# Transformer layers on one core: the expert phase between the two shared halves of each FFN, all routing inside the first half, and no engine loops

## The reference

```python
x = x + 0.5 * _L0_ffn_ref(_layernorm(x, axis=-1), ...)
x = x + _L0_attn_ref(_layernorm(x, axis=-1), ...)
x = x + 0.5 * _L0_ffn_ref(_layernorm(x, axis=-1), ...)
```

```python
xn = xf * jax.lax.rsqrt(jnp.mean(xf * xf, axis=-1, keepdims=True) + eps)
probs = jax.nn.softmax(xn @ router_w.T, axis=-1)
topk_p, topk_i = jax.lax.top_k(probs, K)              # K = 2 of E = 8 experts
order = jnp.argsort(~sel, axis=1, stable=True)
dispatch = order[:, :capacity]                        # 640 slots for each expert
eout = jnp.einsum('eci,eih->ech', gate * up, rd)      # 1024 hidden channels
routed = jnp.zeros_like(xf).at[dispatch.reshape(-1)].add(contrib.reshape(-1, h))
```

## Time and profile before

| | before |
|---|---|
| timed runs, median | 2442.22 us (2438.7 to 2442.6) |
| span of the profiled execution | 2445.0 us |
| PE busy | 2300.4 us (94%) |
| DVE busy | 1379.4 us (56%) |
| POOL busy | 501.5 us (21%) |

### The profile page before, as it was taken

The page is one execution under the profiler, slowest core; times in us unless marked ns, Lnnn a source line. Parts: engine busy times, 40 slices in busy tenths (PEclk is TensorE's granted clock), DMA queues, the critical chain, the costliest instruction groups (busy, mean ns, idle before and its releaser), DMA issues. The chain is left out here.

```text
span 2445.0 us, 42873 instructions
## 1 busy us (share of the span) xinstructions
PE 2300.4 (94%) x14276; PEld 2116.3 (87%) x14276; DVE 1379.4 (56%) x2890; ACT 970.2 (40%) x1940; POOL 501.5 (21%) x614
## 2 busy tenths in 40 slices
PE   7999999998999997788888988999999998999997
PEld 6888888887999997688888877888888887999997
DVE  4554454433666666778777773554454433666663
ACT  3333333332444444545444542333333332544442
POOL 1000003442121122223222220000003443121222
PEclk9999999998999999778787787999999998999999
DMA  6212113422343443100000002212113422343441
GB/s 207 72 59 87 61 57 107 126 81 72 94 104 91 99 99 90 61 1 0 0 0 0 0 1 87 76 56 87 61 57 109 124 80 68 98 103 89 102 92 17
DMA packets 198241, 175.59 MB, mean 72 GB/s; under 512 B 18697, under 2 KB 176829, under 8 KB 198144
## 3 DMA queue, kind: packets, MB, share of 16 engines
q1 hardware_dynamic: 177152, 144.57, 19.4%
q0 software_dynamic: 20992, 29.77, 6.4%
HBM read 108.51 MB, written 72.26 MB: 74 GB/s over the span
## 5 line engine op out<-in xcount | busy, mean ns | idle before, releaser
L340 PE MATMUL gate_p<-zh,w 128*128 128x320 f32 (+1 forms) x2048 | 641.3, 358 | 3.3 <-DVE zl L845 3.3
L340 PE MATMUL quad<-zh,w 128*128 128x320 f32 (+1 forms) x2048 | 628.8, 352 | 0.0
L1032 DVE TENSOR_TENSOR h_s<-quad,sg_s 128x512 f32<-128x512 f32 (+1 forms) x512 | 302.2, 590 | 473.9 <-PE quad L340 467.0
L658 ACT CAST hh<-h_s 128x512 fp32r<-128x512 f32 (+1 forms) x512 | 276.4, 540 | 648.9 <-DVE h_s L1032 648.9
L1040 DVE TENSOR_TENSOR hl<-h_s,hh 128x512 fp32r<-128x512 f32 (+1 forms) x512 | 303.8, 593 | 305.1 <-ACT hh L658 305.1
L649 ACT ACTIVATE sg_s<-gate_p 128x512 f32<-128x512 f32 (+1 forms) x512 | 265.2, 518 | 414.7 <-PE gate_p L340 414.5
L377 PE MATMUL quad<-w,hh 128*128 128x256 f32 x2048 | 410.2, 283 | 3.9 <-DVE hl L1040 3.9
L340 PEld LDWEIGHTS quad<-zh,w 128*128 128x128 f32 x2048 | 375.6, 189 | 44.2
L340 PEld LDWEIGHTS gate_p<-zh,w 128*128 128x128 f32 x2048 | 377.5, 189 | 40.3 <-DVE zl L845 3.7
L340 PE MATMUL gate_p<-zl,w 128*128 128x512 f32 (+1 forms) x1024 | 361.7, 353 | 0.0
L340 PE MATMUL quad<-zl,w 128*128 128x512 f32 (+1 forms) x1024 | 360.0, 352 | 0.0
(11 more groups left out here) (179 smaller groups left out, 3002.1 us busy)
## 6 DMA issues: line engine op xcount, KB each, us to landing
stage<-in_L_ffn_rg SPq DMA_DIRECT2D x128, 128.0 KB, 2.3
stage<-in_L_ffn_ru SPq DMA_DIRECT2D x128, 128.0 KB, 2.4
stage<-in_L_ffn_rd SPq DMA_DIRECT2D x128, 128.0 KB, 2.3
slots_d<-empty SPq DMA_DIRECT2D x16, 662.5 KB, 4.8
xr<-slots_d SPq DMA_DIRECT2D x32, 265.0 KB, 3.0
zh_d<-zh SPq DMA_DIRECT2D x16, 512.0 KB, 3.1
zl_d<-zl SPq DMA_DIRECT2D x16, 512.0 KB, 3.9
zn_d<-zn SPq DMA_DIRECT2D x16, 512.0 KB, 5.1
```

The lines of the kernel that those rows point to most:

```text
L340: last = pe.matmul(dst, a, b, start=(k == 0), stop=(k == 3 * n - 1))
L658: nc.scalar.copy(hh[:, par, 0:ncol], h_s[:, par, 0:ncol]).then_inc(sm["hh_done"], 1)
L1032: v.tensor_tensor(h_s[:, par, 0:ncol], up_p[:, par, 0:ncol], sg_s[:, par, 0:ncol], ALU.mult).then_inc(sm["h_done"], 1)
```

## The change

The phases of each FFN now run in the order `s0`, `e`, `s1`. The preparation of a block is spread over three chunks, so that all eight blocks are prepared by chunk 23 of the 64 chunks of `s0`; blocks 2 to 7 are prepared in separate buffers (`zph`, `zpl`), saved, and loaded back for their own `s0` block. The 15 parts of routing run at chunks 24 to 34 of `s0`, most of them two to a chunk. `scatter` has four row buffers and loads rows three tiles ahead. The expert sums of both FFNs are added in an internal array; `x` is loaded back during `s1`, and `s1` adds its shared half to it. In FFN 2 the finished `x` is then saved as the output. The attention weights are loaded and split, and most padding is cleared, during `s1` of FFN 1; the two value buffers are cleared by POOL after the last down matmul. All loops are written out. The first weights of FFN 2 are split during the last block of `s1`.

```diff
-        PH = {"s0": 0, "s1": NB, "e": 2 * NB}
+        PH = {"s0": 0, "e": NB, "s1": NB + NEB}
+        def prep_at(g):
+            k, r = divmod(g + 2, 3)
+            return (k, ("ln", "rows", "T")[r]) if 1 <= k < NB else (None, None)
+        def router_at(g):
+            k, r = divmod(g - 2, 3)
+            return k if r == 0 and 1 <= k < NB else None
+        ROUTE_M = 30
+        ROUTE = {24: (0,), 25: (1,), 26: (3, 4), 27: (5, 6), 28: (7,), 31: (8, 9), 32: (10, 11), 33: (12, 13), 34: (14, 15)}
...
-                for phase in ("s0", "s1", "e"):
-                    period = 4 if phase == "e" else 2
+                for phase in ("s0", "e", "s1"):
+                    if phase == "e":
+                        row_transposes(f, 0)
...
+                                for part in ROUTE.get(g, ()):
+                                    route(f, part)
+                                if c == 6:
+                                    piece_low(f, 1, b)
...
+            def row_load(f, t):
+                q = t % SROWS
+                wait(pool, scat[q], 32 * (NT // SROWS * f + t // SROWS))
+                g.dma_start(srow[:, q, 0:C], zn_rows[:, t, :]).then_inc(sr_in[q], 16)
+                g.tensor_copy(srow[:, q, C:ROW], table[:, t, :])
+                g.tensor_copy(sidx[:, q, :], slot_i[:, :, t]).then_inc(sm["sidx_in"], 1)
+            def scatter(f):
+                for t in range(SROWS - 1):
+                    row_load(f, t)
+                for t in range(NT):
+                    q = t % SROWS
+                    if t + SROWS - 1 < NT:
+                        row_load(f, t + SROWS - 1)
+                    pool.wait_ge(sr_in[q], 16 * (NT // SROWS * f + t // SROWS + 1))
...
             def attention():
+                pool.wait_ge(sm["down_done"], NCH * FB)
+                g.memset(vh[:, :, :, :].bitcast(F32), 0.0).then_inc(sm["a_const"], 1)
+                g.memset(vl[:, :, :, :].bitcast(F32), 0.0).then_inc(sm["a_const"], 1)
...
+            def shared_phase_1(f):
+                load_z(f, "s1", 1)
+                for par in range(2):
+                    sp.wait_ge(sadd[par], 48 * XB * (f + 1))
+                for b in range(NB):
+                    load_sums(f, b)
+                for b in range(NB):
+                    if b + 1 < NB and b:
+                        load_z(f, "s1", b + 1)
...
+                    if f == 0 and b == NB - 1:
+                        for j in range(NCH):
+                            load_piece(1, 0, j)
+                    if f == 1 and b:
+                        save_out(b - 1)
+                if f == 1:
+                    save_out(NB - 1)
```

More of the change, by code:

```diff
@@ L19 @@
 HD = 16
[L22 to L44, removed]
 def wait(eng, semaphore, value):
-    if not isinstance(value, int) or value > 0:
+    if value > 0:
         eng.wait_ge(semaphore, value)
[L53 to L66, removed]
 def program(nc, x_in, w_qkv, ln_w, w_proj, router_w, rg, ru, rd, sg, su, sd, out):
@@ L253, in program @@
             add("R", "s0", 0)
[L254 to L257, removed]
+            for g in range(NB * NCH):
+                if prep_at(g)[1] == "T":
+                    add("T", "s0", prep_at(g)[0])
+                if router_at(g) is not None:
+                    add("R", "s0", router_at(g))
+                if g == ROUTE_M:
+                    add("M")
             add("T", "e", 0)
@@ L260, in program @@
                 if b:
-                    add("O", "e", b - 1)
+                    add("O", b - 1)
                 if b < NEB - 1:
                     add("T", "e", b + 1)
-            add("O", "e", NEB - 1)
+            add("O", NEB - 1)
         POOL_CONSTS = 12
[L268 to L298, removed]
+        def shared_count(f, phase, b):
+            return 2 * NB * f + {"s0": 0, "s1": NB}[phase] + b + 1
@@ L301, in piece_of, with buf_of @@
         def piece_of(f, unit, j):
             return (f * UNITS + unit) * NCH + j
[L304 to L323, removed]
+        def buf_of(f, unit):
+            return (unit + f) % 2
@@ L325, in program, with unit_of, before @@
+        def unit_of(phase, b):
+            return 0 if phase == "s0" else UNITS - 1 if phase == "s1" else 1 + b // 2
+        def before(phase, b):
+            order = [("s0", i) for i in range(NB)] + [("e", i) for i in range(NEB)] + [("s1", i) for i in range(NB)]
+            at = order.index((phase, b))
+            return order[at - 1] if at else None
         HALF = 8
@@ L606, in attention @@
                 pe.wait_ge(sm["aw_l"], 1)
-                sweep(pe, NT + LEAD + 3, 4, step, head=LEAD + 4, tail=LEAD + 3)
+                for s in range(STEPS):
+                    step(s)
             pe.wait_ge(sm["pool_const"], POOL_CONSTS)
@@ L779, in step @@
                         last.then_inc(sm["a_qc"], 1)
[L781 to L782 removed]
+                act.wait_ge(sm["down_done"], NCH * FB)
+                act.wait_ge(sm["a_pad"], 6)
+                act.wait_ge(sm["a_const"], 4)
+                for s in range(STEPS):
+                    step(s)
             ffn(0)
@@ L1018, in ffn @@
                         first_low(j)
-                for phase in ("s0", "s1", "e"):
-                    period = 4 if phase == "e" else 2
+                for phase in ("s0", "e", "s1"):
+                    if phase == "e":
+                        meta(f, 0)
+                        row_low(f, 0)
                     ncol = EB if phase == "e" else SB
-                    def body(s, phase=phase, ncol=ncol):
-                        hk = hooks(f, phase, s)
-                        last = s.reg is None and s.index == LEN[phase] - 1
+                    for b in range(LEN[phase]):
+                        prev = before(phase, b)
```

1075 lines of the change are left out of this document (512 added, 563 removed).

## The result

The changed kernel took 2537.45 us (median of 4 runs, 2524.75 to 2550.69) beside 2440.93 us of the kernel before: a ratio of 1.0385, 95% interval 1.035 to 1.042. It is 97 us slower; 2411 was forecast. The profiled executions differ by 86.0 us, 11 less than the medians: the four runs of the changed kernel lie 26 us apart, and the profiled one is among the shorter (2532.9 us).

The account below looks back on a forecast made before the run. TensorE, busy 94% of the span, was taken as the bound, so only its idle stretches and clock could give time. 2445.0 - 27.1 - 7.9 - 5.5 + 6.0 + 3.4 = 2413.9, less 2.8 gives 2411 us; range 2398 to 2429.

Parts of the forecast that it names:

- part 1: Scatter under `s0`: tiles of 3.2 to 3.3 us, PE's idle before the expert blocks and its slow clock go, -27.1 us.
- The first rival: Scatter: row loads stay late in an in-order queue, tiles near 5.44 us, 62 us idle per FFN, 2535 us; 5%.
- The slack of 3.44 us a tile: Scatter under `s0`: 106.6 us remain for 31 tile periods, so 3.44 us a tile cost nothing.
- The turning point at 3.9: Scatter: at 3.9 us a tile the stalls of two FFNs eat the 31 us of gain.
- the small stall: Scatter: at 3.5 to 3.7 us a tile PE stalls 2 to 8 us per FFN, 2415 to 2427 us; 10%.
- Slow clock, -7.7: First expert block: full clock once PE's idle stretch before it goes, 3.9 us less in one FFN, -7.7 in both.
- End of FFN 1: From FFN 1's last down matmul to attention: 8.1 us of wait instead of 16.9, -7.9 us in the sum.
- The tail: After the last down matmul: 7.1 us to the end instead of 13.5, transposes moved, -5.5 us.
- Routing: Routing in `s0`: late `lg`, the exp and double parts stall PE about 3.8 us per FFN, +6.0 us in all.
- The clock behind it: After each routing stall: lower granted clock costs 1.7 us per FFN, +3.4 us in all.
- Loops and attention, 0: Attention and written-out loops: no change in time, though attention's clock could shift it 10 us either way.
- the rival's 6 us: Attention: removing loops saves 0.3 us in each of about 20 steps, 6 us, 2405 us; 8%.

Follow-up runs that it names:

- lead2: The changed kernel with row loads two tiles ahead instead of three, on the same four buffers: ratio 0.9897 to the kernel before.
- behind: The changed kernel, loads still three tiles ahead but each issued behind the tile's two indirect DMAs: ratio 0.9893 to the kernel before.
- eight: The changed kernel with eight row buffers and loads seven tiles ahead: ratio 1.0257 to the kernel before.
- dose: lead2 with one more clearing of 265 elements on POOL in each tile: ratio 1.0001 to the kernel before.
- before3: The kernel before with three row buffers and loads one tile ahead, all else untouched: ratio 0.9875, repeated 0.9902 and 0.9863.
- group: The changed kernel with rows loaded four tiles at a time into two buffers of four: ratio 0.9856 to the kernel before.
- group_route: group with routing parts 1 to 15 and the exp one chunk later: ratio 0.9852 to the kernel before, 0.9799 when repeated.
- zlate: group_route with the `zh` and `zl` load for `s1` behind the last expert block's second weight piece: ratio 1.0104, repeated 0.9793 and 0.9916.
- early: zlate with the first expert rows transposed and split in chunk 62 of `s0`: ratio 1.0065, repeated 1.0014 and 0.9954.

## Why the prediction was wrong

**The step that failed** is in part 1: "With loads three tiles ahead that wait should go. I take 3.2 to 3.3". The wait for the load did go; I did not ask which buffer the load goes into. Four buffers and three ahead mean the buffer of the previous tile. The sum priced the wait for the landing of the indirect DMAs at nothing, though the trace of before had it: 2.7 us from issue to landing. The tile took 5.29 us, of which 2.05 are this wait, and PE waited 113.1 us for `xr` where the forecast had 0. lead2, behind and eight show that the distance between a load and the last use of its buffer did it.

**The first rival** gave 2535 us, and 2537 came. That it came so close is in part luck. Its mechanism was wrong: it blamed a queue that serves in order, and that was refuted by lead2. Its price for the idle time was near, 124 us for 113, as the landing of a buffer's last transfers (2.05) happens to cost about what the load had (2.24). In spans it gave 2413.9 + 124 = 2537.9 for 2531.0: 11 us too much for the waits and 4 for all other terms, against 8 of slow clock that it took as gained. Its chance of 5% was too small, as the buffer's reuse could be read from the change (in POOL's order the load ahead of the send from buffer 2 waits for `scat1`, one tile behind). The slack of 3.44 us a tile was right: (5.29 - 3.44) x 31 = 57.4, and PE waited 57.6. The turning point at 3.9 came out too (dose: 3.92 to 3.97, ratio 1.000), but with other terms off in both directions, as below.

**The tile without waits**: 3.2 to 3.3 forecast, 3.34 when quiet and 3.6 on average (lead2). Even with the right distance 4 to 5 us of wait stay; I priced that as the small stall.

**Slow clock, -7.7**: not gained in the changed kernel, as every wait for `xr` profiled here had a slow clock behind it; before3 and group gained most of it once the wait was zero.

**End of FFN 1**: -7.9 forecast, -9.7 measured. POOL clears 2112 elements in 1.86 us, not 2.6; DVE had taken 1.82. My bound from the row of 265 elements took a fixed part for a rate. By the ratio that the Trainium skill has (GPSIMD Engine Reference, section 3.1, Elementwise) the estimate was 3.6; the page speaks of an addition, and for a clearing this trace has POOL as fast as DVE.

**The tail**: -5.5 forecast, -7.9 measured; 4.7 us from the last down matmul to the end for 7.1. The save, issued at 2527.53, landed in 3.0 us as forecast; it is the close behind it that took 0.5 us and not 2.7.

**Routing**: 3.8 us per FFN forecast, 2.7 and 2.6 measured, and 0.57 and 0.58 before where I had taken 0.8: +4.2 for +6.0. The late `lg` and the exp are the cause, as group_route shows; the double parts, which I charged 1.1 us, cost no wait of their own. The clock behind it: 1.1 us once, none the other time, for 3.4.

**Not seen**: the load of `zh` and `zl` on SyncE holds back a weight piece in the last expert block, and PE waits 1.2 and 2.2 us. In zlate_again, with the load later, no wait is left there.

**Loops and attention, 0**: attention took 501.1 for 500.2 us, and the waits for `k_t` are 23.6 for 23.8. Given attention's own spread (486 to 516 us), the first pair can't exclude the rival's 6 us; the second speaks against it. The rule of the Trainium skill on taken branches (Runtime: NRT & Kernel Launch, section Instruction fetch mechanics) changed nothing here that can be seen.

With a scatter that doesn't wait, the rest of the change pays where no gaps come: on one chip group_route and zlate reach 0.980 and 0.979, where the scatter alone on the old order reaches 0.990. On the two chips with gaps zlate and early lie at 0.992 to 1.010, and before3 had none anywhere.

## What to carry to other kernels

When a load is issued ahead, ask two distances: how far ahead of its use it is, and how long ago its buffer was last read. With n buffers and a lead of n-1 the second is one step, whatever n is; a lead of n-2, or the load placed behind the step's own reads, gives it one step more for nothing. And a stretch that is moved under cover needs its time per item times the number of items worked out with all its waits, that for a buffer to come free among them: here 0.5 us a tile decided between gain and loss.

## What was unexpected of the hardware

Attention's time goes with a granted clock that settles differently from run to run of like programs. Windows of group and of group_route, the same work:

```profile
959.60:1451.90 492.30, 418.65 (x2753) 389.72 (x2753) 383.17 (x812) 243.59 (x545) 135.88 (x160) 0.82 0.00 1
```

```profile
955.80:1471.60 515.80, 448.33 (x2752) 418.34 (x2752) 378.31 (x812) 243.72 (x545) 135.60 (x160) 0.77 0.00 1
```

24 us lie between them, at 0.82 and 0.77 of full clock; over all profiled runs it was 486 to 516 us. What settles it was not shown. It hides differences of under 0.5% in the total, which the span less attention shows. The gaps of PE during the scatter, 24 to 53 us, in some kernels and on some chips only, are the other surprise.
